# A decoder in two streams: new written orders in which each engine takes the streams' steps

## The reference

```python
x = _layernorm(x + _L0_attn_ref(x, L0_attn_W_qkv, L0_attn_W_out), axis=-1)
x = _layernorm(x + _L0_xattn_ref(x, ctx_1024, ...), axis=-1)
x = _layernorm(x + _L0_ffn_ref(x, ...), axis=-1)
...
x = _layernorm(x + _L3_ffn_ref(x, L3_ffn_weight, L3_ffn_bias), axis=-1)
```

## Time and profile before

| what | value |
|---|---|
| three runs | 1021.28, 1022.54, 1025.13 us; median 1022.54 |
| profiled execution: span | 1020.0 us (no separate time of it is given; the median lies 2.5 us above) |
| TensorE busy | 904.2 us, 89% |
| weight loads busy | 700.2 us, 69% |
| VectorE, ScalarE, GpSimd busy | 539.7, 450.7, 50.8 us |
| instructions | 22561 |

### The profile page before, as it was taken

The page is one execution under the profiler, slowest core; times in us unless marked ns, Lnnn a source line. Parts: engine busy times, 40 slices in busy tenths (PEclk is TensorE's granted clock), DMA queues, the critical chain, the costliest instruction groups (busy, mean ns, idle before and its releaser), DMA issues. The chain is left out here.

```text
span 1020.0 us, 22561 instructions
## 1 busy us (share of the span) xinstructions
PE 904.2 (89%) x9368; PEld 700.2 (69%) x9368; DVE 539.7 (53%) x1569; ACT 450.7 (44%) x923; POOL 50.8 (5%) x71
## 2 busy tenths in 40 slices
PE   7689899999989998997987979989998989899772
PEld 5257768778778785666556757867887868686441
DVE  5733565653265575347636853655325547454345
ACT  2044343453454673574255233244465446433442
POOL 2300000010010000001000000001001000000000
PEclk8799989999999998999999999999999999999965
DMA  9100000401000301103000000040000030000000
GB/s 344 40 2 3 1 1 1 166 2 37 2 19 1 141 3 40 43 12 139 2 12 1 2 1 2 2 166 33 6 1 19 1 140 1 2 1 2 2 1 21
DMA packets 6838, 36.12 MB, mean 35 GB/s; under 512 B 721, under 2 KB 4305, under 8 KB 5458
## 3 DMA queue, kind: packets, MB, share of 16 engines
q1 hardware_dynamic: 6738, 34.68, 9.1%
HBM read 34.15 MB, written 0.52 MB: 34 GB/s over the span
## 5 line engine op out<-in xcount | busy, mean ns | idle before, releaser
L673 PE MATMUL bank<-xT,weights_F 128*128 128x256 f32 x832 | 202.9, 386 | 3.1 <-ACT p L1818 2.6
L673 PEld LDWEIGHTS bank<-xT,weights_F 128*128 128x128 f32 x832 | 152.0, 193 | 26.8 <-issue 4.2
L681 PEld LDWEIGHTS bank<-weights_F,p 128*128 128x128 f32 x1088 | 133.4, 191 | 18.8 <-DVE p L1363 7.2
L681 PE MATMUL bank<-weights_F,p 128*128 128x128 f32 x1088 | 141.3, 278 | 3.7 <-DVE p L1363 3.0
L1743 ACT ACTIVATE p<-bank 128x512 f32<-128x512 f32 x160 | 84.5, 601 | 121.0 <-PE bank L492 120.9
L1683 ACT ACT_TABLE_LOAD x76 | 97.5, 1283 | 12.9 <-DMA weights_con<-in_con 5.9
L1347 DVE SCALAR_TENSOR_TENSOR res<-bank,comb,res 128x128 f32<-128x128 f32 x184 | 55.7, 345 | 74.1 <-PE bank L681 71.6
L1184 DVE TENSOR_REDUCE m_wide<-bank 128x4 f32<-128x512 f32 x96 | 60.3, 684 | 43.4 <-PE bank L780 33.5
L1818 ACT ACTIVATE p<-bank 128x512 f32<-128x512 f32 x72 | 42.5, 597 | 91.6 <-PE bank L673 91.2
L1363 DVE TENSOR_TENSOR p<-p,bank 128x512 f32<-128x512 f32 x72 | 49.3, 685 | 47.5 <-PE bank L673 27.3
L1894 ACT ACTIVATE p<-bank 128x512 f32<-128x512 f32 x64 | 36.6, 598 | 51.3 <-PE bank L673 51.2
(11 more groups left out here) (319 smaller groups left out, 1356.0 us busy)
## 6 DMA issues: line engine op xcount, KB each, us to landing
weights_F<-in_L1f SPq DMA_DIRECT2D x2, 4096.0 KB, 13.8
weights_F<-in_L0f SPq DMA_DIRECT2D x2, 3456.0 KB, 13.4
weights_F<-in_L2f SPq DMA_DIRECT2D x2, 3456.0 KB, 12.1
weights_Y<-in_L1x_kv SPq DMA_DIRECT2D x2, 1024.0 KB, 10.6
weights_Z<-in_L1x SPq DMA_DIRECT2D x2, 1024.0 KB, 12.9
weights_Y<-in_L2a SPq DMA_DIRECT2D x2, 898.0 KB, 4.4
weights_Z<-in_L2x SPq DMA_DIRECT2D x2, 449.0 KB, 3.2
weights_L3m<-in_L3m SPq DMA_DIRECT2D x2, 288.0 KB, 6.1
```

Source lines behind the costliest of these rows:

```text
L673: m = mm(b[:, k * NT:(k + 1) * NT], W[weight][:, f:f + P], s.xT[:], start=True, stop=True)
L681: m = mm(b[:, tk(u)], h[:, tk(u)], w, start=k == 0, stop=k == len(chunks) - 1)
```

## The change

`TURN_ORDER` has new strings for all five engines, and four waits stand a step later. No instruction of a stream is added or taken away, but for loads of tables, whose number follows from the order. Of the strings only the lines around the stretches at 195 us and 757 us, and those of SyncE, are shown; all the others differ too.

```diff
 TURN_ORDER = {
     "pe":
...
-        "a2 b3 a2 b1 a2 b2 a2 b1 a4 b4 a1 b2 a1 b1 a1 b2 a2 b1 a1 b4 a1 b1 a4 b1 a3 b1 a3 b1 a1 b1 a3 b1 a1 b1 a1 "
...
-        "a2 b1 a1 b1 a13 b1 a1 b1 a1 b1 a4 b1 a1 b1 a2 b2 a2 b1 a1 b3 a2 b8 a1 b1 a1 b1 a1 b2 a1 b2 a1 b5 a1 b4 "
...
+        "b2 a1 b2 a1 b3 a1 b2 a3 b1 a1 b1 a1 b3 a1 b3 a1 b1 a2 b2 a4 b1 a1 b1 a2 b5 a1 b1 a3 b1 a2 b1 a2 b1 a1 b1 "
...
+        "a3 b3 a1 b1 a2 b1 a3 b1 a1 b1 a3 b1 a1 b1 a6 b1 a6 b3 a1 b1 a2 b1 a1 b1 a1 b1 a1 b2 a1 b7 a1 b1 a1 b4 a1 "
...
     "sp":
-        "a3 b6 a18 b12 a23 b26 ",
+        "a2 b1 a1 b1 a9 b3 a5 b5 a3 b2 a1 b1 a3 b1 a1 b2 a2 b1 a3 b1 a1 b2 a2 b1 a2 b3 a1 b1 a1 b1 a1 b1 a1 b1 a1 "
+        "b10 a2 b4 a2 b2 ",
 }
...
                     yield
-                    pe.wait_ge(*ready("L1x_kv"))
                     for c in range(0, 8, 2):
                         yield
+                        if c == 0:
+                            pe.wait_ge(*ready("L1x_kv"))
                         by_feature("L1x", f"k{c}", "act", *((W["L1x_kv"][:, (c + k) * P:(c + k + 1) * P], s.ctxT[:]) for k in range(2)))
...
                 def L1x():
-                    pe.wait_ge(*freed("L1a", "xT"))
-                    pe.wait_ge(*ready("L1x"))
                     for c in range(0, 8, 2):
                         yield
+                        if c == 0:
+                            pe.wait_ge(*freed("L1a", "xT"))
+                            pe.wait_ge(*ready("L1x"))
                         by_feature("L1x", f"q{c}", "act", *((W["L1x_q"][:, (c + k) * P:(c + k + 1) * P], s.xT[:]) for k in range(2)))
...
                     if queries is not None:
+                        dve.wait_ge(*freed(st, "q"))
                         spread_heads(s.bd_q, queries, sem("queries"))
...
                 def L2x():
-                    dve.wait_ge(*freed("L2x", "q"))
                     yield
                     yield from softmax("L2x", s.qT)
...
                 def rest(then=None):
 
-                    pool.wait_ge(*told("x_new", NS))
+                    done = told("x_new", NS)
                     if then:
+                        pool.wait_ge(*done)
                         then()
                     yield
```

More of the change, by code:

```diff
@@ L145 @@
     "pe":
[11 rows of a table removed]
-    "dve":
[10 rows of a table removed]
-    "act":
[8 rows of a table removed]
[13 rows of a table added]
+    "dve":
[12 rows of a table added]
+    "act":
[11 rows of a table added]
     "pool":
-        "a1 b1 a1 b2 a3 b1 a1 b1 a1 b1 a3 b1 a1 b2 a1 b2 a1 b1 a4 b1 a2 b4 a1 b2 a2 b2 a1 b1 a3 b1 a1 b2 a1 b2 a1 "
-        "b2 a2 b2 a1 b1 ",
+        "b1 a2 b2 a2 b1 a1 b1 a1 b1 a5 b4 a3 b1 a3 b4 a1 b1 a2 b3 a1 b2 a1 b1 a4 b3 a1 b2 a1 b1 a2 b2 a1 b1 a1 b1 ",
     "sp":
-        "a3 b6 a18 b12 a23 b26 ",
+        "a2 b1 a1 b1 a9 b3 a5 b5 a3 b2 a1 b1 a3 b1 a1 b2 a2 b1 a3 b1 a1 b2 a2 b1 a2 b3 a1 b1 a1 b1 a1 b1 a1 b1 a1 "
+        "b10 a2 b4 a2 b2 ",
 }
```

## The result

The changed kernel takes 1040.24 us (median of 4 runs) against 1021.91 (4 runs of the kernel before on the same chip): a ratio of 1.0183, with a 95% interval of 1.0151 to 1.0214. That is 18.3 us slower, where the prediction had 14.2. The profiled execution's span is 1038.3 us, 18.3 above that of before. In the changed kernel the lines that the text names stand 7 to 10 lower (L834 is L843, L458 is L465, L1465 is L1475, L1517 is L1527).

The account below looks back on a forecast made before the run. TensorE, busy 904.2 of 1020.0 us, sets the time. Terms 2.3 - 2.7 + 2.9 + 3.5 + 6.5 - 2.6 + 4.3 = +14.2 on 1022.5 gave 1036.7 us; own range 1029 to 1046, reaching down to 1013 for 8 in 10.

Parts of the forecast that it names:

- What isn't touched in cost: Whole kernel: no matmul gets longer; the four later waits and SyncE's new DMA order cost 0.
- 757 to 785 us, +6.5: TensorE waits 2.37 us before b's second L834 numerators, then 4.1 at a's L458 behind L1517; ends +2.4 and +6.5.
- 200 us, +3.5: Stream a in L1x: +2.4 before L834's second numerators, +1.9 for b's L745, some 0.8 back at L843; ends 0, +4.3.
- 125 us, -2.7: The 5.0 us wait at L726 is filled by b's steps, though short pauses come back; ends -5.0 and 0.
- 142 to 182 us, +2.9: b's SiLU steps go ahead of a's evictions on ScalarE: 1.9 us plus some 1.0; TensorE has 0.4 us slack.
- The clock, 0 in the sum: Filled wait near 125 us may give back 3.5 us, new wait at 775 may take as much; 3.5 either way.
- Start, +2.3: First 60 us: b's steps go ahead of leading stream a's, making a 3.1 us late before some comes back; ends 0, 3.1.
- The rest, +4.3: Waits of about 1 us at 292-345, 536-612, 612-755 us and single places; half of 8.6 taken, ends 0 and 8.6.
- gains elsewhere, -2.6: -1.3 at 376 to 404 us, a bank of a freed earlier; -1.3 in the last stretch, a's tail ahead of b's.
- The signs: Expected: about 2.4 us waits at L834, about 4 at L458, L726's gone, 70 table loads, TensorE's busy time same, span longer.
- no change: Rival: whole kernel stays at 1022.5 us, each delay made good at the next pause; chance 0.17.
- the tables: Rival: 70 table loads instead of 76, mainly near 225 and 740 us, save 7.9 us; about 1013 us; chance 0.17.

Follow-up runs that it names:

- experiment 1: Changed kernel with the old orders of TensorE, VectorE and ScalarE, keeping the four later waits and SyncE's and GpSimd's new orders: 1022.41 us, ratio 1.0003.
- Experiment 6: Changed kernel with five of stream a's steps on ScalarE and VectorE moved ahead of b's at 270 to 297 us, TensorE's order untouched: 1033.34 us, ratio 1.0110.
- experiment 9: Kernel before with the three compute engines' new orders at 121 to 188 and 940 to 1005 us: both 0.9960, first alone 0.9992, second alone 0.9972.
- experiment 2: Changed kernel with the old orders of TensorE, VectorE and ScalarE at 268 to 297 and 755 to 785 us: 1026.59 us, ratio 1.0049.
- experiment 7: Changed kernel with six table loads put back as reloads, two near 355 us and four near 740 us: 1043.69 us, ratio 1.0206.

## Why the prediction was right

The sum was 4 us short of the measured 18.3, and the mechanism is the forecast one: TensorE's work is unchanged and waits were made where it had had other work. That the total came so near is in part luck, as the terms show. Going through the steps:

- **What isn't touched in cost** was right: experiment 1 has a ratio of 1.0003. Two of its reasons were not. A second, short wait for a DMA stands in the trace before (L561 behind xT_in, 0.8 us; 1.1 after). And single matmuls do get longer, such as L465 with 1.19 us for 0.71; only their sum stays, 904.9 us for 904.2.
- **757 to 785 us, +6.5:** measured +6.1 in the traces and +6.0 as a kernel of its own (+7.7 in that one's trace). The second wait was taken as 4.1 and is 3.66, plus slower matmuls behind it. The first was taken as 2.4 and is 1.37. What was wrong is that the second numerators need both L1465. They go into two banks, and TensorE starts when the first is free.
- **200 us, +3.5:** +2.9. The same error in the first half. For the second, TensorE waits 0.8 us at b's product of scores instead of 1.9 (3.8 less 1.97 is 1.8):

```profile
200.95 2.15 PE L843 MATMUL bank<-p,vz 128*64 128x128 f32 x32 [1.37 <-DVE p L1475]
...
206.73 1.12 PE L752 MATMUL bank<-wide,qk 32*128 32x512 f32 x2 [0.81 <-DVE p L1438]
```

- **270 to 297 us, no term:** the largest miss, +6.4. The list of large terms left this stretch out, although ScalarE's and VectorE's strings hold the same pattern as at 757 us. Experiment 6 shows it.
- **125 us, -2.7 and 142 to 182 us, +2.9:** -3.8 and +1.4. The sum of both was put 2.6 us too high. The filled wait is real in the trace; in the whole kernel it is not resolved (experiment 9).
- **The clock, 0 in the sum:** both movements that were named are in the rows. Before, 120 to 142 us had 0.84 and 755 to 785 us had 1.00; after (the number behind the busy times is the clock), the filled stretch has 1.00 and the one with the new wait 0.95:

```profile
120.00:138.00 18.00, 13.24 (x124) 10.00 (x117) 13.26 (x47) 6.52 (x16) 0.73 (x1) 1.00 0.00 1
...
769.00:802.00 33.00, 27.00 (x305) 22.93 (x304) 13.03 (x33) 11.54 (x25) 1.70 (x3) 0.95 0.01 1
```

- **Start, +2.3:** 0. By 25 us the delay is 1.5 us, then it is gone. Before, a's masked scores (the second row is the mask, the third the scores) run at about half the speed after a wait of 2.02 us; after, at full speed behind a wait of 1.98:

```profile
27.33 1.86 PE L486 MATMUL bank<-neg_causal_bf,ident_bf 128*128 128x512 bf16 x4 [2.02 <-DVE mx L1192]
29.12 1.83 PE L488 MATMUL bank<-wide,qk 32*128 32x512 f32 x8
```

```profile
28.74 1.02 PE L493 MATMUL bank<-neg_causal_bf,ident_bf 128*128 128x512 bf16 x4 [1.98 <-DVE mx L1201]
29.69 1.14 PE L495 MATMUL bank<-wide,qk 32*128 32x512 f32 x8
```

So the 0 owes something to faster matmuls. In the traces of experiments 2, 6 and 7, which have the new order here, the first 61 us have +1.0, +0.5 and +2.4; in the eight traces with the old order they have -2.4 to +4.3. The term is not resolved.

- **The rest, +4.3, and gains elsewhere, -2.6:** 536 to 592 us was sized +1.0 and has +6.7 in the traces, the end was sized -1.3 and has -6.1. The two nearly cancel, and so do the misses at the start and at the first crossing in part. The total came out closer than its terms.
- **The signs:** the wait at L458 is there with its size and the waits at L834 are there with 1.37 us, not 2.4. The wait at L726 has shrunk and isn't gone.
- **The rivals:** no change and the tables both fall. The saved loads are in the trace, and the kernel is slower all the same. The switch of 1.31 us is measured behind a GELU: L1894 belongs to L1f, and the kernel has table sets for two kinds of GELU besides the two named. Nine loads went and not six, and the six put back in experiment 7 cost some 3.5 us in its trace: the rival was too high in its price, not without ground. The Trainium skill's page "ScalarE: Activation LUTs" has the rule to batch calls of activation functions by table set (section "Table sets: the hidden batching unit"). Experiment 7 bears it out in part: a load costs TensorE something where a SiLU or GELU that it waits for is behind it.

Two terms were not tested alone: 536 to 592 us, and the small ones from 297 to 535. But the traces of experiments 2, 6 and 7 have the new orders there, too, and eight have the old ones. From 536 to 592 us the new orders have +7.2, +8.3 and +7.2, the old ones 0.0 to +2.0; from 297 to 376 us the new ones have +3.5, +3.5 and +4.8 (the last with two loads put back there), the old ones 0.0 to +1.7. So both losses are the orders'; which of the moved steps make them is not shown. From 404 to 535 us the new orders have -2.1 to +2.9 and the old ones -1.7 to +4.9: the +2.9 of the table is not shown to come from the order.

## What to carry to other kernels

With a written order on in-order engines, ask at each place where two streams cross what the bounding engine does while the other engines make its next input: a round trip is free only while the other stream's work stands between. A step that waits behind the other stream is easily overlooked in the queue of an engine that is half idle (VectorE with 52%, ScalarE with 42%), because nothing in its busy share shows it. Check every occurrence of a pattern, and in both turns; the one that was left out here was as dear as the one that was found.

## What was not expected of the hardware

TensorE's granted clock differs between executions of one order in the same stretch. Experiment 1 has the old orders of the compute engines, and from 536 to 560 us it shows 0.79 where the kernel before shows 0.93 (the last figures are the clock, the DMAs' share and GB/s). First the kernel before, then experiment 1:

```profile
536.00:560.00 24.00, 18.38 (x208) 15.07 (x207) 15.75 (x70) 12.30 (x31) 1.01 (x3) 0.93 0.00 1
```

```profile
536.00:560.00 24.00, 20.46 (x205) 16.10 (x197) 15.95 (x66) 10.95 (x26) 1.47 (x4) 0.79 0.00 1
```

TensorE's delay between these two traces changes by 1.4 to 1.7 us in such stretches, though the orders of the compute engines are the same. The stretch holds TensorE's waits at the end of L3x and L0x (2.24 us at L458 is the longest before), and the matmuls there run at one of the two speeds seen in the fences on the start.

Larger differences are there, too: with the old orders, the traces of experiment 9 differ from the kernel before by up to 4.9 us from 404 to 535 us, and by 3.4 us from 785 to 944 us (the L673 shown there). So two traces tell a local difference of a few us only if a wait stands beside it or if other traces repeat it, as they do at both crossings and from 536 to 592 us. A single kernel's runs here spread over 10 us (1018.13 to 1028.10 in 29 runs of the kernel before).
